# Early-fusion block on one NeuronCore: ranking read from PSUM, layer-norm normalisations on ScalarE, token grid in one instruction, new orders

## The reference

```python
h = concat([tok(x), txt])                   # two-level Haar wavelet, resized to 8x8 tokens, @ W + b
h = h + self_attention(_layernorm(h))       # q = k = v, one head
h = h + routed_mlp(_layernorm(h))           # 64 -> 256 -> 64, gelu; only the top-ranked tokens
h = h + window_attention(_layernorm(h))     # 16 query heads, 1 kv head, RoPE, RMS norm, window of 128
h = h + expert_ffn(_layernorm(h))           # argmax over 32 experts, 64 -> 16 -> 64
```

```python
weights = (x @ wr + br)[..., 0]             # one number for each token: the router's output
_, idx = top_k(weights, s // 2)             # rank within the sequence of 192 (ties: lower index first)
sel = x[idx[:s // 2 - 1]]
y = (gelu(sel @ w1 + b1) @ w2 + b2) * w_sel # added back to the selected tokens only
```

## Time and profile before

| | |
|---|---|
| three runs | 585.87, 580.71, 582.63 us |
| median | 582.63 us |
| profiled execution | 583.62 us, its span 581.8 us |
| mean granted TensorE clock | 0.971 |
| busy, share of the span | PE 86%, DVE 72%, ACT 54%, POOL 40% |

### The profile page before, as it was taken

How to read it: one execution, slowest core, us unless ns; L and a number is a source line. 1 busy time by engine, 2 the same in 40 slices (tenths; PEclk the granted TensorE clock), 3 DMA queues, 4 the chain that set the end, 5 groups by cost and what they waited for, 6 DMA issues and landing times.

```text
span 581.8 us, 14569 instructions
## 1 busy us (share of the span) xinstructions
...
## 2 busy tenths in 40 slices
...
DMA packets 6450, 6.29 MB, mean 11 GB/s; under 512 B 4208, under 2 KB 5744, under 8 KB 6256
## 3 DMA queue, kind: packets, MB, share of 16 engines
...
...
## 4 chain that ended last, share of the span: by engine, by line
PE 47%; DVE 35%; ACT 9%; POOL 2%; issue 2%; DMA 2%; SPq 1%; POOLq 0%; ACTq 0%; DVEq 0%
PE bank L961 38%; PE bank L979 10%; DVE eq L515 5%; DVE negm L631 4%; DVE q_sb L568 4%; DVE ssq L585 4%; DVE tb L568 4%; DVE on L648 3%; ACT qT L810 3%; POOL qs L793 2%; DMA p<-masks 2%; DVE eq L506 1%; ACT qs L810 1%; DVE eq L431 1%; DVE rec L644 1%
## 5 line engine op out<-in xcount | busy, mean ns | idle before, releaser
L631 DVE TENSOR_REDUCE negm<-bank 128x2 f32<-128x384 f32 (+1 forms) x128 | 79.2, 619 | 39.6 <-PE bank L961 38.4
L793 POOL TENSOR_TENSOR qs<-q_sb,qs 128x1024 fp32r<-128x1024 f32 x24 | 56.8, 2368 | 107.8 <-ACT qs L810 107.8
L919 ACT ACTIVATE p<-bank 128x512 f32<-128x512 f32 x112 | 66.0, 599 | 56.6 <-PE bank L961 55.4
L961 PE MATMUL bank<-kh,qT 128*128 128x128 f32 (+1 forms) x384 | 82.0, 323 | 0.0
L810 ACT ACTIVATE qT<-bank 128x512 fp32r<-128x512 f32 x96 | 54.3, 596 | 50.3 <-PE bank L979 49.9
L961 PE MATMUL bank<-vx,p 128*64 128x65 f32 x1536 | 68.8, 225 | 1.3 <-DVE on L648 1.2
L961 PEld LDWEIGHTS bank<-vx,p 128*64 128x64 f32 x1536 | 60.5, 138 | 13.9 <-issue 6.8
L756 POOL TENSOR_TENSOR q_sb<-q_sb,tb 128x512 f32<-128x512 f32 x24 | 36.5, 1519 | 74.3 <-DVE tb L568 74.3
L961 PEld LDWEIGHTS bank<-kh,qT 128*128 128x128 f32 x384 | 64.2, 199 | 2.1
L961 PE MATMUL bank<-sh_r,sh_l 128*128 128x512 f32 x112 | 53.2, 475 | 0.0
L644 DVE RECIPROCAL rec<-bank 128x4 f32<-128x4 f32 (+1 forms) x88 | 15.7, 179 | 48.4 <-PE bank L961 48.0
...
## 6 DMA issues: line engine op xcount, KB each, us to landing
...
sh_r<-mT SPq DMA_DIRECT2D x32, 4.0 KB
...
```

Source lines behind the costliest of these rows:

```text
L631: ve.tensor_reduce(dst, src, AX_X, ALU.max, negate=True).then_inc(s_vec, 1)
L793: gp.tensor_tensor(qs[:, :, D:2 * D], ta[:, t, 0:NH, :], qs[:, :, 0:D].bitcast(F32), ALU.subtract).then_inc(b_pool, 1)
L919: ac.activation(dst.rearrange("s h t -> s (h t)"), bank[BANK_E[n % 2]][:, :], ACT.Exp).then_inc(e_act, 1)
L961: return pe.matmul(dst, lhsT, rhs, start=start, stop=stop, skip_group_check=True)
```

## The change

1. Token grid. `cols` on PE becomes four matmuls (96 rows, 32 columns of weights, 16 columns moved), each into its own 32 partitions; DVE makes the grid with one instruction over 128 partitions. The constant `resize` has 32 columns and no longer 128.
2. The normalisations of layer norms 1, 2 and 4 are ScalarE activations (`Identity` with scale = the reciprocal root and bias = minus mean times it), three each, in new ACT steps `xn1`, `xn2` and `D.ln`. POOL makes the bias with two more operations in each of them, one ahead of the two that it had (mean times -1) and one behind (times the root, `shift`). What waited for DVE's normalisation waits for ACT's. Two small DVE operations of norm 1 (`xpad`) and all of norm 3 stay on DVE.
3. Ranking reads bank 4. The ACT copy `rt` is gone; the bias `br` is a further row of the router's weights, against a row of ones in `xaT`. `h1a` on PE waits for `rank3`'s count, and in the A stream `rank1`, `rank2`, `rank3` stand ahead of `h1a`.
4. All `MERGE` strings are new; two lines of one of them stand in the diff.

The diff, its constants and lists of names cut:

```diff
 WEIGHT_AT, WEIGHT_N = offsets(WEIGHT_COLS)
-A_VEC = ["grid", "tok", "sums1", "stats1", "xn1", "recip", "ctx", "sums2", "stats2", "xn2", "wcol", "equal", "rank", "wsel",
+A_VEC = ["grid", "tok", "sums1", "stats1", "pad", "recip", "ctx", "sums2", "stats2", "wcol", "equal", "rank", "wsel",
          "y", "yw", "h"]
-A_POOL = ["var1", "rstd1", "var2", "rstd2", "hx"]
+A_POOL = ["var1", "rstd1", "shift1", "var2", "rstd2", "shift2", "hx"]
 A_PE = ["rows", "cols", "tok", "xT1", "s01", "s2", "ctx", "xT2", "route", "h1a", "h1b", "y"]
-A_ACT = ["rows", "xT1", "p01", "p2", "xT2", "route", "h1a", "h1b"]
+A_ACT = ["rows", "xn1", "xT1", "p01", "p2", "xn2", "xT2", "h1a", "h1b"]
 B_VEC = (["sums", "stats", "xn", "hi", "xs", "r00", "r01", "ssq00", "r10", "ssq01", "r11", "ssq10", "r20", "ssq11",
...
     + [f"S{n}" for n in range(8, 16)] + ["mT2"]
-A_ORDER = ["rows", "cols", "tok", "ln1", "xn1", "xT1", "s01", "s2", "ctx", "ln2", "xn2", "xT2", "route", "rank1", "h1a", "rank2", "h1b",
-           "rank3", "y", "h"]
+A_ORDER = ["rows", "cols", "tok", "ln1", "xn1", "xT1", "s01", "s2", "ctx", "ln2", "xn2", "xT2", "route", "rank1", "rank2", "rank3", "h1a",
+           "h1b", "y", "h"]
 W_ORDER = ["eye", "shr0", "mask", "shr1", "wq", "shr2", "shr3"]
...
-    "pe": "A15 B4 A B A B A B A B A2 B2 A2 B2 A S A B A B S A S B S B2 S A S B A S E2 S B2 A S B2 V S B A S B V S B "
...
+    "pe": "A15 B3 A B A B2 A B A B A2 B2 A B2 A S B2 S A S B A S B2 A S B A S E S E V B2 S B2 A V B S B2 S E S E V A "
...
         def _(ve):
-            ve.memset(xaT[D:P, :], 0.0)
+            ve.memset(xaT[D:P, :], 0.0).then_inc(set_ones, 1)
+            ve.wait_ge(set_ones, 1)
+            ve.memset(xaT[D:D + 1, :], 1.0)
             ve.memset(xdT[D:P, :], 0.0)
...
                 ve.wait_ge(a_pe, after(A_PE, p, "cols"))
-                f = bank[BANK_A][:, 0:2 * 32].rearrange("m (b o i) -> m b o i", b=2, o=4)
-                for o in range(4):
-                    m = slice(32 * o, 32 * o + 32)
-                    ins = ve.tensor_tensor(grid[m, :, :, :], f[m, :, o, :].unsqueeze(3).broadcast_to([32, 2, 8, 8]),
-                                           cs("own_j")[m, :].unsqueeze(1).unsqueeze(1).broadcast_to([32, 2, 8, 8]), ALU.mult)
-                ins.then_inc(a_vec, 1)
+                f = bank[BANK_A][:, 0:16].rearrange("m (b i) -> m b i", b=2)
+                ve.tensor_tensor(grid, f.unsqueeze(3).broadcast_to([P, 2, 8, 8]),
+                                 cs("own_j").unsqueeze(1).unsqueeze(1).broadcast_to([P, 2, 8, 8]), ALU.mult).then_inc(a_vec, 1)
             def a_tok(p):
...
                 ve.wait_ge(a_pool, after(A_POOL, p, "rstd1"))
-                normalise(xa, h0[:, p.n, :, :], mvA, rsA, None)
                 for b in range(2):
...
                 stats(sumsD, mvD, d_vec)
-            def d_xt(p):
-                ve.wait_ge(stored[p.par], p.half * (16 * OUT_DMAS))
-                ve.wait_ge(d_pool, after(D_POOL, p, "rstd"))
-                normalise(o_sb[p.par], hC, mvD, rsD, d_vec)
-
             def d_logits(p):
...
                 gp.tensor_tensor(rs[:, :], rs[:, :], minus_half[:, :], ALU.pow).then_inc(sem_pool, 1)
+            def shift(nm, mv, rs, sem_pool, names, p, rstd_name):
+
+                gp.wait_ge(sem_pool, after(names, p, rstd_name))
+                gp.tensor_tensor(nm[:, :], nm[:, :], rs[:, :], ALU.mult).then_inc(sem_pool, 1)
+
             def a_ln1(p):
                 gp.wait_ge(a_vec, after(A_VEC, p, "stats1"))
+                if p.n > 0:
+                    gp.wait_ge(a_act, after(A_ACT, p, "xn2") - len(A_ACT))
+                gp.tensor_tensor(nmA[:, :], mvA[:, :, 0], minus_one[:, :], ALU.mult)
                 rstd(mvA, rsA, a_pool, A_POOL, p, "var1")
+                shift(nmA, mvA, rsA, a_pool, A_POOL, p, "rstd1")
             def a_ln2(p):
                 gp.wait_ge(a_vec, after(A_VEC, p, "stats2"))
+                gp.tensor_tensor(nmA[:, :], mvA[:, :, 0], minus_one[:, :], ALU.mult)
                 rstd(mvA, rsA, a_pool, A_POOL, p, "var2")
+                shift(nmA, mvA, rsA, a_pool, A_POOL, p, "rstd2")
             def a_hx(p):
-                gp.wait_ge(a_vec, after(A_VEC, p, "xn2"))
+                gp.wait_ge(a_act, after(A_ACT, p, "xn2"))
                 gp.tensor_tensor(hx[:, :, :], h0[:, p.n, :, :], xf[:, :, :], ALU.add).then_inc(a_pool, 1)
...
                 gp.wait_ge(d_vec, after(D_VEC, p, "stats"))
+                gp.tensor_tensor(nmD[:, :], mvD[:, :, 0], minus_one[:, :], ALU.mult)
                 rstd(mvD, rsD, d_pool, D_POOL, p, "var")
+                shift(nmD, mvD, rsD, d_pool, D_POOL, p, "rstd")
...
             bA, bD, bO = bank[BANK_A], bank[BANK_D], bank[BANK_O]
+            def normalise(dst, src, rs, nm, done):
+
+                for t in range(NT):
+                    ins = ac.activation(dst[:, t, 0:D], src[:, t, :], ACT.Identity, scale=rs[:, t:t + 1], bias=nm[:, t:t + 1])
+                ins.then_inc(done, 1)
+
+            def a_xn(dst, k):
+                def f(p):
+                    ac.wait_ge(a_pool, after(A_POOL, p, f"shift{k}"))
+                    if k == 1 and p.n > 0:
+                        ac.wait_ge(a_vec, p.n * len(A_VEC))
+                    if k == 2 and p.n > 0:
+                        ac.wait_ge(a_pool, p.n * len(A_POOL))
+                    normalise(dst, h0[:, p.n, :, :], rsA, nmA, a_act)
+                return f
+
+            def d_xn(p):
+                ac.wait_ge(stored[p.par], p.half * (16 * OUT_DMAS))
+                ac.wait_ge(d_pool, after(D_POOL, p, "shift"))
+                normalise(o_sb[p.par], hC, rsD, nmD, d_act)
+
             def a_do(name, dst, src, func=ACT.Copy, **kw):
                 def f(p):
-                    if p.n == 0 and name[0] == "route":
+                    if p.n == 0 and name[0] == "h1a":
                         ac.wait_ge(ld_w, 16)
...
                 ("A", "rows"): a_do(["rows"], z_sb, bA[0:IMG, 0:2 * 32]),
+                ("A", "xn1"): a_xn(xa, 1), ("A", "xn2"): a_xn(xf, 2), ("D", "ln"): d_xn,
                 ("A", "xT1"): a_do(["xT1"], xaT[0:D, :], bA[0:D, 0:PT]),
...
                 ("A", "xT2"): a_do(["xT2"], xfT[0:D, :], bA[0:D, 0:PT]),
-                ("A", "route"): a_do(["route"], rt[:, :, :].rearrange("q b t -> q (b t)"), bA[:, 0:2 * T], ACT.Identity,
-                                     bias=wt("br")),
                 ("A", "h1a"): a_h1(0), ("A", "h1b"): a_h1(1),
...
                 for b in range(2):
-                    ins = mm(bA[0:IMG, 32 * b:32 * b + 32], img[p.par][:, b, :], cs("resize")[0:IMG, 0:32], True, True)
+                    ins = mm(bA[0:IMG, 32 * b:32 * b + 32], img[p.par][:, b, :], cs("resize")[0:IMG, :], True, True)
                 ins.then_inc(a_pe, 1)
...
                 pe.wait_ge(a_act, after(A_ACT, p, "rows"))
-                halves(bA[:, 0:2 * 32], cs("resize")[0:IMG, :], z_sb, True, True).then_inc(a_pe, 1)
+                z = z_sb.rearrange("c (b o i) -> c b o i", b=2, o=4)
+                for o in range(4):
+                    ins = mm(bA[32 * o:32 * o + 32, 0:16], cs("resize")[0:IMG, :], z[:, :, o, :], True, True)
+                ins.then_inc(a_pe, 1)
             def a_tok(p):
...
                 def f(p):
-                    wait_apart(pe, a_vec, after(A_VEC, p, wait))
+                    wait_apart(pe, a_act, after(A_ACT, p, wait))
                     transposes(bA, [src[:, t, 0:D] for t in range(NT)], ident, a_pe)
...
                 pe.wait_ge(a_act, after(A_ACT, p, "p2"))
+                pe.wait_ge(a_vec, after(A_VEC, p, "pad"))
                 w = D + 1
...
                 def f(p):
-                    pe.wait_ge(a_act, after(A_ACT, p, ["route", "h1a"][c]))
+                    if c == 0:
+                        pe.wait_ge(a_vec, after(A_VEC, p, "rank"))
+                    else:
+                        pe.wait_ge(a_act, after(A_ACT, p, "h1a"))
                     halves(bA[:, 0:PT], wt("w1")[:, P * c:P * c + P], xfT[:, :], True, True).then_inc(a_pe, 1)
...
     c["w2"] = w["L0_ffn_w2"].reshape(2, P, D).transpose(1, 0, 2).reshape(P, 2 * D)
-    c["wr"] = rows(np.repeat(w["L0_ffn_wr"], P, 1))
-    c["br"] = np.repeat(w["L0_ffn_br"].reshape(1, 1), P, 0)
+    c["wr"] = rows(np.repeat(np.concatenate([w["L0_ffn_wr"], w["L0_ffn_br"].reshape(1, 1)], 0), P, 1))
     c["b1"] = w["L0_ffn_b1"].reshape(2, P).T
```

More of the change, by code:

```diff
@@ L38 @@
 SHAPE_COLS = dict(rope=192, iota=32, before=384)
-FIRST_COLS = dict(ident=128, resize=128, own_j=8, tok=64, tokb=64)
-WEIGHT_COLS = dict(wo01=512, wo2=512, w1=256, w2=128, wr=128, br=1, b1=2, b2=64, qn=64, kn=64,
+FIRST_COLS = dict(ident=128, resize=32, own_j=8, tok=64, tokb=64)
+WEIGHT_COLS = dict(wo01=512, wo2=512, w1=256, w2=128, wr=128, b1=2, b2=64, qn=64, kn=64,
                    rout=32, rb=32, e1=512, e2=256, e2b=64)
@@ L69 @@
     + [f"tq{t}{i}" for t in range(NT) for i in range(4)]
-D_VEC = ["h", "sums", "stats", "xn", "logits", "top", "index", "indexf", "onehot", "off", "out"]
-D_POOL = ["var", "rstd"]
```

(21 more changed lines are left out.)

4 lines of the change are left out of this document (2 added, 2 removed), and 63 rows, old and new, of the table MERGE.

## The result

562.17 us, median of four runs from 561.68 to 564.69, against 582.89 us for the kernel before (580.71 to 585.87): the ratio is 0.9654, with a 95% interval from 0.9615 to 0.9694. The kernel became 3.5% faster; 2.7% was forecast. The profiled execution took 561.68 us with a span of 559.9.

A forecast was written before the change was run, and what follows sets the result against it. PE was taken as the bound, busy 58.24 of 60.70 us in the steady part. From 583.6 us, steady -10.7, fill -5.0, start +1.0 and end -0.5 gave 568.4, so a median of 567 us, range 553 to 580.

The forecast's parts named there:

- The bound and the stall: Steady part: PE busy 58.24 of 60.70 us is the bound; L515's two SBUF inputs wait for GpSimd, 3.0 us of stall.
- Ranking from PSUM: rank2 and rank3 on DVE read the bank, so the 3.0 us stall and X2's wait for the division should go.
- X2's wait: PE's wait for DVE's division `on` before X2, 8.7 us in five steady pairs, 1.7 a pair, expected to go at most.
- the three falls: Drops of PE's clock to about half speed after X2 in the steady part, 1.25 us each, 3.8 in all, to go.
- I charge 0.3 ... 0.6 a pair: New PE waits: 0.3 us a pair for ranking's tight places, 0.6 for normalisations on ScalarE; 4.5 us over five steady pairs.
- They are off PE's path where DVE has slack: The nine normalisations DVE loses, 2.8 us a pair, were said not to hold PE where DVE has slack.
- Worth nothing itself: Gelus side by side: 12 fewer table loads, 15.4 us of ACT, none on PE's path in the steady part; only makes room.
- Start "+1.0": Start of the kernel: ranking before h1a +3.3, shifts +0.6, grid -0.9, stalled L454 -1.6, norm 1 -0.4: +1.0 us.
- fill "-5.0": Stretch 68 to 128.7: DVE waits of 2.5, 1.6 and 1.2 and one fall of 1.25 go, 1.5 of new waits: -5.0 us.
- End: "-0.5, its waits being mostly for other things": End of the kernel: 0.5 us less, its waits mostly for other things and the last expert chain longer by 0.5.

The follow-up runs named there:

- ranking_from_copy: The changed kernel with ScalarE copying the router output to SBUF again, ranking reading that copy and h1a waiting for the copy, not rank3: 562.54 us, ratio 0.9689.
- before_v7_first: The kernel before with one edit in six pairs: on VectorE the division of V7 stands ahead of rank2, not behind it; 572.03 us, ratio 0.985.
- norms_on_dve: The changed kernel with a pair's nine normalisations back on VectorE and without GpSimd's two extra operations: 568.66 us, ratio 0.9784.
- exp_between_gelus: The changed kernel with an unused one-column exponential on ScalarE ahead of each pair's second gelu, bringing table loads back: 569.3 us, ratio 0.9813.

## Why the prediction was right, and where not

The number, 562.2 us, lies in the range that was stated, 5 us under the forecast. Not all of that is merit: the terms behind it missed both ways.

**The bound and the stall: right, and the cause is shown.** PE's busy time set the period, 57.7 of 58.4 us. That the second SBUF operand makes L515 wait for GpSimd is shown by ranking_from_copy and the changed kernel in the same order, 2404 ns against 424. A case inside the changed kernel's own trace:

```profile
...
64.92 4.08 POOL L790 TENSOR_TENSOR q_sb<-q_sb,ny 128x1024 f32<-128x1024 f32 x2
```

```profile
...
67.91 1.50 DVE L512 SCALAR_TENSOR_TENSOR eq<-bank,wcol,cst 128x192 f32<-128x192 f32 x4
...
71.02 1.67 DVE L523 SCALAR_TENSOR_TENSOR wsel<-rank,wcol 128x3 f32<-128x3 f32 x1
```

Rank2 from the bank runs unstalled beside L790 in its 4.08 us; L523, with both inputs in SBUF, takes 1.67 us beside the next GpSimd instruction, and 0.16 in the earlier trace rows. The count of SBUF inputs isn't the whole rule: L454 has one tensor from SBUF, and in the kernel before one of them took 1939 ns beside an L786 of 1.90 us, part of the 2.52 us in the earlier trace rows.

**"Ranking from PSUM ... with it X2's wait, at most 8.7 us, and the three falls": the amount right, the credit wrong.** The waits and falls went. But before_v7_first takes X2's wait and the falls away by one swap, 1.5%, with the stall in place. In the new order rank2 isn't stalled even from the copy; there PSUM reading saves the copy ahead of rank1, 0.5 us a pair, which its own two early waits take back. Four kernels with the new orders make a table of two by two:

| | ranking from the copy | ranking from the bank |
|---|---|---|
| norms on VectorE | 573.12 | 568.66 |
| norms on ScalarE | 562.54 | 562.17 |

So reading the bank is worth 4.5 us while VectorE normalises, and nothing that can be told once it doesn't. What I read as one cause was two conditions: a stall, and X2 behind it. Taking X2's division out from behind the stall is enough. That ending the stall alone would be enough as well is not shown: no run reads the bank in the old order.

**"I charge 0.3 ... 0.6 a pair": the mis-sized term.** It put 4.5 us of new waits into the steady part in place of 11.4 old ones. PE's waits there are 2.9 us in all, and negm's had been 1.6 before; what can be new is 1 us or so. The five pairs, before and after:

```profile
...
128.70:435.90 307.20, 294.57 (x3701) 231.49 (x3701) 255.66 (x796) 194.45 (x370) 143.44 (x125) 0.98 0.02 5
```

```profile
...
125.30:417.50 292.20, 288.52 (x3721) 226.73 (x3720) 228.26 (x736) 189.70 (x403) 148.18 (x156) 1.00 0.02 5
```

PE's idle time fell by 8.95 us, where the forecast had 6.9; 1.1 of it is a wait for `xdT` that the forecast left out. Balanced places held: rank1 begins at 239.47 and X2 at 242.45, PE waiting 0.19. PE's busy time fell by 6.05 us. The three falls account for 3.8 by the forecast's price. The other 2.3, some half a microsecond a pair, had no term, and no run here isolates it.

**"They are off PE's path where DVE has slack": wrong.** norms_on_dve costs 0.8 us a pair. VectorE's share of 84% hid that, in the orders of that experiment, norms 4, 3 and 1 meet within 5 us shortly ahead of the score maxima; that this meeting is the cause is read from the trace and not tested by itself. I had looked for what the move might cost on ScalarE, where three activations take 1.10 us and I had put 0.9, and nobody in the steady part waits for them:

```profile
...
207.55 1.09 ACT L834 ACTIVATE o_sb<-hC,nmD,rsD 128x64 f32<-128x64 f32 x3
...
210.82 1.11 ACT L834 ACTIVATE xa<-h,nmA,rsA 128x64 f32<-128x64 f32 x3
```

The estimate of 1.06 us by the Trainium skill (ScalarE: Activation LUTs, "Rules for kernel authors") was the nearer one. Its rule to keep such work on VectorE agrees with the single instructions here, 0.75 us for three against 1.10, but not with the kernel's time, by norms_on_dve.

**"Worth nothing itself" for the tables: wrong.** exp_between_gelus costs 0.9 us a pair. The Trainium skill (ScalarE: Activation LUTs, "Rules for kernel authors") says to group by table set, and exp_between_gelus agrees that it pays. The loads are 17 now and 29 before, each 1283 ns. Its budget of 2.7 us for a switch to a different set is more than these traces show: in exp_between_gelus the activation behind a load starts 1.3 us after the load does (252.25 and 253.54).

**Start "+1.0", fill "-5.0": the sum came near, in part by luck.** h1a begins 3.2 us later behind `route` than before, as forecast (it waits 3.93 us; +3.3 forecast). h1b then waits 2.0 us and not 0.7, because the gelu table, formerly loaded during the first matmuls, is now loaded after them: a term I left out. Rows of the second pair's images begin at 39.8, before at 35.1. But at the second pair's `route` (65.5, before 65.0) only 0.5 of these 4.7 us are left, and at its first q transposes (72.8 in both) none. The grid, norm 1 and the stalled L454, all forecast, can account for part of what came back; the rest I can't place. From there to the first X2 it is 52.5 us and was 55.9. That is 3.4 less and not 5.0, as PE still waits 1.9 us for `on` and now 2.2 for `qs`, which had been 0.8.

**End: "-0.5, its waits being mostly for other things".** It gave 3.5. Waits for `qs`, `on`, `qT` in the last pairs went from 1.8, 1.8 and 0.9 to 0.2, 0.2 and none. Two went the other way. One is new, for the masks that SP moves, for which I had put no term. The other is the expert chain's, 0.5 by the forecast and 0.7 in the traces. Before, then after:

```profile
...
PE bank L979 <- DVE o_sb L454: 3.4, 1, 3.4
```

```profile
...
PE bank L987 <- DMA sh_r<-mT: 1.5, 1, 1.5
```

```profile
...
PE bank L1005 <- ACT o_sb L834: 4.1, 1, 4.1
```
